# Moving a projection and early routing from the banks of the sum y to a transposing bank, in the first stage of an eight-layer kernel

## The reference, cut to what matters

```
xn = norm(norm(x)); u, z = split(xn @ W_in)
u2 = silu(conv(u)); dt, B, C = from(u2 @ W_xp)
for each of 16 states n and 256 channels e, along the 1024 tokens:
    h = exp(dt*A[e,n]) * h + (dt*u2)*B[n]        # a scan
    y += h * C[n]
y = (y + u2*D) * silu(z)
x = x + xn0 + res * (y @ W_out)                  # xn0: x normalised once
logits = norm(x) @ wg.T -> softmax, top groups, top 4 of 32 experts
```

## Time and profile before

| | us |
|---|---|
| three executions | 1595.17, 1598.65, 1599.42 |
| the profiled execution's own time | 1595.64 |
| its span (what the trace covers) | 1593.8 |
| the scan loop, first scan to the start of the last | 79.1 to 273.0 |
| VectorE busy in the span | 1022.7 |
| GpSimd busy in the span | 694.3 |
| TensorE busy in the span | 1259.4 |

### The profile page before, as it was taken

How to read it: one execution, slowest core, us unless ns; L and a number is a source line. 1 busy time by engine, 2 the same in 40 slices (tenths; PEclk the granted TensorE clock), 3 DMA queues, 4 the chain that set the end, 5 groups by cost and what they waited for, 6 DMA issues and landing times.

```text
span 1593.8 us, 27288 instructions
## 1 busy us (share of the span) xinstructions
PE 1259.4 (79%) x10086; PEld 895.2 (56%) x10086; DVE 1022.7 (64%) x1915; ACT 789.9 (50%) x1629; POOL 694.3 (44%) x688
## 2 busy tenths in 40 slices
PE   5888989322776568877868669998999999985996
PEld 2577768312554234444446534455776777874996
DVE  7798986760111888878743554547976885642775
ACT  3788685210433237767742235555665565321442
POOL 1099996474666340001014330024870881043453
PEclk9689999655888669999979889998999999997999
DMA  6388692112221431211001141112000003001113
GB/s 220 122 263 304 219 339 104 33 49 65 79 78 50 172 130 54 68 43 47 17 16 34 56 158 55 35 37 75 1 1 1 1 1 159 1 29 46 46 45 99
DMA packets 75492, 133.48 MB, mean 84 GB/s; under 512 B 12755, under 2 KB 39830, under 8 KB 74720
## 3 DMA queue, kind: packets, MB, share of 16 engines
q1 hardware_dynamic: 66432, 115.45, 22.1%
q0 software_dynamic: 8064, 13.87, 2.7%
q10 hardware_dynamic: 864, 2.43, 0.4%
HBM read 95.70 MB, written 38.38 MB: 84 GB/s over the span
## 4 chain that ended last, share of the span: by engine, by line
PE 47%; issue 18%; DVE 13%; ACT 7%; POOL 6%; DMA 4%; SPq 4%; another core or an unknown queue 1%; POOLq 0%; DVEq 0%; ACTq 0%
PE ps L1907 6%; PE ps L4138 3%; POOL sb_arena L1072 3%; PE ps L2274 2%; DVE sb_arena L1973 2%; ACT sb_arena L2221 2%; PE ps L2257 2%; PE ps L2516 1%; PE ps L3219 1%; PE ps L4105 1%; PE ps L4106 1%; PE ps L4107 1%; PE ps L3190 1%; SPq L68 1%
## 5 line engine op out<-in xcount | busy, mean ns | idle before, releaser
L1973 DVE TENSOR_REDUCE sb_arena<-ps 128x2 f32<-128x1024 f32 (+2 forms) x192 | 211.4, 1131 | 56.9 <-PE ps L2502 31.9
L2221 ACT ACTIVATE sb_arena<-ps 128x512 f32<-128x512 f32 (+1 forms) x320 | 160.3, 554 | 56.3 <-PE ps L2274 52.6
L889 DVE TENSOR_TENSOR_SCAN sb_arena<-ps,sb_arena 128x1024 f32<-128x1024 f32 x64 | 144.1, 2279 | 13.6 <-ACT ps L980 12.7
L2005 POOL CAST sb_arena<-sb_arena 128x8 bf16<-128x8 f32 (+2 forms) x32 | 6.5, 203 | 287.4 <-DVE sb_arena L1973 146.1
L1907 PE MATMUL ps<-sb_arena 128*32 128x256 f32 (+3 forms) x1856 | 115.1, 355 | 0.4 <-ACT sb_arena L2455 0.2
L1633 POOL DMA_INDIRECT y<-sb_arena x80 | 77.7, 972 | 55.7 <-ACT sb_arena L1582 32.9
L1173 POOL DMA_INDIRECT xe<-sb_arena x80 | 79.7, 996 | 49.9 <-issue 29.1
L1072 POOL TENSOR_TENSOR sb_arena<-sb_Wreg,sb_arena 128x1024 f32<-128x1024 f32 x32 | 74.8, 2365 | 59.9 <-DMA sb_arena<-bcrows 51.4
L705 PE MATMUL ps<-sb_const,sb_arena 128*128 128x128 f32 x768 | 92.3, 278 | 0.0
L705 PEld LDWEIGHTS ps<-sb_const,sb_arena 128*128 128x128 f32 x768 | 90.2, 195 | 2.0 <-issue 2.0
L2274 PE MATMUL ps<-sb_arena 51*128 51x256 bf16 (+2 forms) x768 | 60.7, 249 | 28.7 <-ACT sb_arena L2221 28.0
(11 more groups left out here) (526 smaller groups left out, 3491.0 us busy)
## 6 DMA issues: line engine op xcount, KB each, us to landing
sb_arena<-bcrows SPq DMA_DIRECT2D x80, 512.0 KB, 6.6
xe<-sb_one SPq DMA_DIRECT2D x31, 260.0 KB, 6.7
sb_Wreg<-e0w SPq DMA_DIRECT2D x24, 256.0 KB, 7.6
sb_arena<-xe SPq DMA_DIRECT2D x16, 325.0 KB
y<-sb_zero SPq DMA_DIRECT2D x20, 256.0 KB, 6.6
sb_arena<-y SPq DMA_DIRECT2D x4, 1024.0 KB, 8.9
sb_Wreg<-e1w SPq DMA_DIRECT2D x16, 256.0 KB, 2.8
sb_Wreg<-e3gu SPq DMA_DIRECT2D x1, 4096.0 KB, 14.2
```

What stands on the lines that cost most here:

```text
L889: e.tensor_tensor_scan(self.hh[i % 3], k.pair(2 * (i % 2)).rearrange("p c t -> p (c t)"), self.dB[i % 3], 0.0, MUL, ADD).then_inc(S.scan.s ...
L1973: e.tensor_reduce(dst, src, AX.X, MAX).then_inc(S.mxr.sem, 1)
L2221: e.activation(self.PT[s % 4][:, 2 * h:2 * h + 2, 0:n], bank[:, :, 0:n], ACT.Exp, scale=self.scale).then_inc(S.ex.sem, 1)
```

## The change

The projection of batch 0 is cut in two halves of four token tiles. Each half goes into bank 4, behind the first half of a transposed item: at i = 35 behind item 34 and at i = 39 behind item 38. VectorE takes each half out at i = 36 and i = 40. The next stage's turns (i = 47, 51) and logits (i = 55, 59) are cut in two in the same way and use bank 4. `turn_h` of items 36, 40, 48, 52, 56 and 60 waits until bank 4 has been read. `start_y` no longer waits for any of it. The signal `op` now counts three projections in place of two; the weights' wait in SyncE's queue goes from 1 to 2. The square root goes from i = 40 to 41, VectorE's part of the normalisation from 42 to 43, ScalarE's from 44 to 45.

```diff
@@ sp
                 w.wait_ge(S.gate, 2)
-                w.wait_ge(S.op, 1)
+                w.wait_ge(S.op, 2)
                 load_w_part(k, e, "e0", i - 38)
@@ turn_h
         before = i - 1 if i % 4 else i - 2
+        if i in (36, 40):
+            w.wait_ge(S.ox, (i - 32) // 4)
+        if i in (48, 52, 56, 60):
+            w.wait_ge(self.after.S.fxa, (i - 40) // 4)
         for c in range(2):
@@ start_y
         w.wait_ge(S.gate, g)
-        w.wait_ge(S.ox, b if eb == 0 else 0)
-        if g == 3:
-            w.wait_ge(self.after.S.fxa, 4)
@@ project_out becomes two functions
+    def project_first(self, e, w, c):
+        k, S = self.k, self.S
         w.wait_ge(S.g_wout, 16)
-        w.wait_ge(S.gate, 2 * b + 2)
+        w.wait_ge(S.gate, 2)
+        self.wait_half(w, 34 + 4 * c, 0)
+        for j in range(4 * c, 4 * c + 4):
+            for eb in range(2):
+                t = e.matmul(k.b(self.C)[:, (j % 4) * 128:(j % 4 + 1) * 128], self.sz[0][:, eb, j * 128:(j + 1) * 128], self.wout[:, eb, :],
+                             start=eb == 0, stop=eb == 1)
+        t.then_inc(S.op.sem, 1)
+    def project_last(self, e, w):    # as project_out(1) before, in banks 6 and 7
...
@@ pe, in the loop over i
             if n == 3 and i > 3:
-                w.wait_ge(S.gate, i // 16)
-                if i == 35:
-                    self.project_out(e, w, 0)
-                if i == 51:
-                    self.after.early_turns_pe(e, w)
-                    self.after.early_logits_pe(e, w)
                 self.start_y(e, w, i // 16)
+            if i in (35, 39):
+                self.project_first(e, w, (i - 35) // 4)
+            if i in (47, 51):
+                self.wait_half(w, i - 1, 0)
+                self.after.early_turns_pe(e, w, (i - 47) // 4)
+            if i in (55, 59):
+                self.wait_half(w, i - 1, 0)
+                self.after.early_logits_pe(e, w, (i - 55) // 4)
+            if n == 3 and i > 3:
                 self.add_y(e, w, i - 3)
             if i > 1 and (n != 2 or i == 2):
                 self.add_y(e, w, i - 2)
@@ out_dve becomes two functions
+    def out_first_dve(self, e, w, c):
+        k, S = self.k, self.S
+        xs = k.Xt[:, c * 512:(c + 1) * 512]
+        w.wait_ge(S.op, c + 1)
+        w.wait_ge(S.res, 16)
+        e.scalar_tensor_tensor(xs, k.b(self.C), k.s("res"), xs, MUL, ADD).then_inc(S.ox.sem, 1)
+        w.wait_ge(S.ox, c + 1)
+        tile_stats(k, e, w, range(4 * c, 4 * c + 4), S.stats if c else None)
...
@@ dve, in the loop over i
-            if i == 35:
-                self.out_dve(e, w, 0)
-            if i == 42:
+            if i in (36, 40):
+                self.out_first_dve(e, w, (i - 36) // 4)
+            if i == 43:
                 self.after.early_norm_dve(e, w)
@@ act, in the loop over i, behind decay(i + 2) and ahead of times_act(i)
-            if i == 40:
+            if i == 41:
                 self.after.deviations_act(e, w, 0)
-            if i == 44:
+            if i == 45:
                 self.after.early_norm_act(e, w)
-            if i == 51:
-                self.after.early_features_act(e, w)
-            if i == 52:
-                self.after.early_logits_act(e, w)
+            if i in (47, 51):
+                self.after.early_features_act(e, w, (i - 47) // 4)
+            if i in (55, 59):
+                self.after.early_logits_act(e, w, (i - 55) // 4)
...
```

More of the change, by code:

```diff
@@ L487, in __init__ @@
             B0=176, B1=176, B2=192, B3=192, B4=160, B5=160, C0=128, C1=128, hT=96, dA=64, dB=64, scan=64, hcv=16, hca=64, hcp=16, acc=64,
-            yd=4, gate=4, op=2, ox=2)
+            yd=4, gate=4, op=3, ox=3)
         k.g_x += [S.B2, S.B3]
@@ L491, in __init__ @@
         self.ready = (S.stats, 6)
-        self.ends = [(S.op, 2), (S.stats, 6), (S.res, 16), (S.dB, 64), (S.hcp, 16)]
+        self.ends = [(S.op, 3), (S.stats, 6), (S.res, 16), (S.dB, 64), (S.hcp, 16)]
     def two(self, v):
@@ L684, in start_y @@
         t.then_inc(S.yd.sem, 1)
-    def project_out(self, e, w, b):
+    def project_first(self, e, w, c):
         k, S = self.k, self.S
         w.wait_ge(S.g_wout, 16)
-        w.wait_ge(S.gate, 2 * b + 2)
+        w.wait_ge(S.gate, 2)
[7 more added lines that the diff above has]
+        k, S = self.k, self.S
+        w.wait_ge(S.gate, 4)
         for j in range(8):
             for eb in range(2):
-                t = e.matmul(k.b(self.Y + j // 4)[:, (j % 4) * 128:(j % 4 + 1) * 128], self.sz[b][:, eb, j * 128:(j + 1) * 128], self.wout[:, eb, :],
+                t = e.matmul(k.b(self.Y + j // 4)[:, (j % 4) * 128:(j % 4 + 1) * 128], self.sz[1][:, eb, j * 128:(j + 1) * 128], self.wout[:, eb, :],
                              start=eb == 0, stop=eb == 1)
@@ L764, in pe @@
         self.after.count_pe(e, w, 0)
-        self.project_out(e, w, 1)
+        self.project_last(e, w)
     def stats_dve(self, e, w, c):
@@ L843, in gate_dve, with out_last_dve @@
         e.tensor_tensor(self.two(zs), self.two(zs), k.pair(self.Y), MUL).then_inc(S.gate.sem, 1)
-    def out_dve(self, e, w, b):
+    def out_first_dve(self, e, w, c):
         k, S = self.k, self.S
-        xs = self.two(k.Xt[:, b * 1024:(b + 1) * 1024])
-        w.wait_ge(S.op, b + 1)
+        xs = k.Xt[:, c * 512:(c + 1) * 512]
+        w.wait_ge(S.op, c + 1)
         w.wait_ge(S.res, 16)
+        e.scalar_tensor_tensor(xs, k.b(self.C), k.s("res"), xs, MUL, ADD).then_inc(S.ox.sem, 1)
+        w.wait_ge(S.ox, c + 1)
+        tile_stats(k, e, w, range(4 * c, 4 * c + 4), S.stats if c else None)
+    def out_last_dve(self, e, w):
+        k, S = self.k, self.S
+        xs = self.two(k.Xt[:, 1024:2048])
+        w.wait_ge(S.op, 3)
         e.scalar_tensor_tensor(xs, k.pair(self.Y), k.s("res"), xs, MUL, ADD).then_inc(S.ox.sem, 1)
-        w.wait_ge(S.ox, b + 1)
-        tile_stats(k, e, w, range(8 * b, 8 * b + 8), S.stats)
+        w.wait_ge(S.ox, 3)
+        tile_stats(k, e, w, range(8, 16), S.stats)
     def dve(self, e, w):
@@ L900, in dve @@
         self.after.disp.dve(e, w, 0)
-        self.out_dve(e, w, 1)
+        self.out_last_dve(e, w)
         self.after.norm_dve(e, w)
@@ L1203, in __init__ @@
         self.S = S = k.signals(
-            g_w=16, stats=4, sd=2, rstd=3, xnv=8, tp=4, fxa=6, **dispatch_signals(4), lg=3, shift=4, probs=4,
+            g_w=16, stats=4, sd=2, rstd=3, xnv=8, tp=4, fxa=7, **dispatch_signals(4), lg=4, shift=4, probs=4,
             scat=1024, smg=4, smu=4, ssg=4, shs=4, sdn=4, sx=4,
@@ L1280, in features, with early_turns_pe, early_logits_pe @@
         return (self.early_xnT if c < 2 else self.xnT)[:, 512 * (c % 2):512 * (c % 2 + 1)]
-    def early_turns_pe(self, e, w):
-        k, S, Y = self.k, self.S, self.before.Y
+    def early_turns_pe(self, e, w, c):
+        k, S = self.k, self.S
         w.wait_ge(k.g_const, 16)
         w.wait_ge(S.fxa, 1)
[L1287 to L1292, removed]
+        for j in range(4):
+            t = e.transpose(k.b(self.before.C)[:, j * 128:(j + 1) * 128], self.early_xn[:, 4 * c + j, :], k.c("ident"))
+        t.then_inc(S.tp.sem, 1)
+    def early_logits_pe(self, e, w, c):
         k, S, E = self.k, self.S, self.E
-        w.wait_ge(S.fxa, 3)
-        for i in range(8):
-            t = e.matmul(k.b(self.before.Y)[:, i * E:(i + 1) * E], self.early_xnT[:, i * 128:(i + 1) * 128], k.s("wgT"), start=True, stop=True)
+        w.wait_ge(S.fxa, 2 + c)
+        for i in range(4 * c, 4 * c + 4):
+            t = e.matmul(k.b(self.before.C)[:, i % 4 * E:(i % 4 + 1) * E], self.early_xnT[:, i * 128:(i + 1) * 128], k.s("wgT"), start=True, stop=True)
         t.then_inc(S.lg.sem, 1)
@@ L1310, in logits_pe @@
         for c in (2, 3):
-            w.wait_ge(S.fxa, c + 3)
+            w.wait_ge(S.fxa, c + 4)
             for j in range(4):
@@ L1405, in route_dve @@
         if h < 2:
-            w.wait_ge(S.fxa, 4)
+            w.wait_ge(S.fxa, 5)
             w.all([(self.before.S.scan, 64), (self.before.S.hcv, 16), (self.before.S.hca, 64), (self.before.S.hcp, 16)])
         else:
-            w.wait_ge(S.lg, h)
+            w.wait_ge(S.lg, h + 1)
         w.mark(e.tensor_reduce(mx, l3, AX.X, MAX))
@@ L1534, in early_norm_act, with early_features_act, early_logits_act @@
         t.then_inc(S.fxa.sem, 1)
-    def early_features_act(self, e, w):
+    def early_features_act(self, e, w, c):
         S = self.S
[L1538 to L1542, removed]
+        w.wait_ge(S.tp, c + 1)
+        e.copy(self.features(c), self.k.b(self.before.C)).then_inc(S.fxa.sem, 1)
+    def early_logits_act(self, e, w, c):
         S = self.S
-        w.wait_ge(S.lg, 1)
-        e.copy(self.early_lg, self.k.b(self.before.Y)[:, 0:256]).then_inc(S.fxa.sem, 1)
+        w.wait_ge(S.lg, c + 1)
+        e.copy(self.early_lg[:, 128 * c:128 * c + 128], self.k.b(self.before.C)[:, 0:128]).then_inc(S.fxa.sem, 1)
     def features_act(self, e, w):
```

## The result

The change made the kernel slower: 1597.24 us, the median of 21 executions, against 1591.26 us for the kernel before (21 executions). The ratio is 1.0046, with a 95% interval of 1.0028 to 1.0063: 4.5 to 10.0 us, 7.3 in the middle; the two medians differ by 5.98. The forecast was +5.0 us, 1602.2 on the base that was then known; the base of these executions is lower, so the shift is what is compared. The profiled execution of the change took 1603.64 us (span 1601.8), that of before 1595.64 (span 1593.8).

A forecast was written before the change was run, and what follows sets the result against it. The prediction took GpSimd to pace the scan loop, so its idle times count. Terms -9.8 + 13.3 + 1.5 = +5.0 us, set on a mean of 1597.2, gave 1602.2 us, range 1594 to 1609.

The forecast's parts named there:

- The stall at 51: GpSimd's idle times from bank borrowing at item 51 go: 9.8 us gained, bounds 7 and 9.8.
- The release: SyncE's queue, held from load_b(39) on, is let go by the projection's second half at 197.2, 13.3 us later.
- What GpSimd pays: GpSimd waits for late B rows after dB(38), dB(42) at 213.7 not 200.33: 13.3 us lost, bounds 9 and 14.
- Crowding: Second-half statistics, square root, norm and ScalarE's tiles at items 40 to 45 delay scans 48, 49: 1.5 us lost, bounds 0 and 5.
- TensorE's clock: TensorE idles about 199 to 211 us and restarts slowly, up to 4 us, left within the bound of 5.
- The sum: Shift at the scan loop's end: -9.8 + 13.3 + 1.5 = +5.0 us, bounds -0.8 to +12.
- The rival that the release costs nothing: Op 2 comes before about 188 us and both stalls go: 12.7 us gained, 1584.5; chance 0.12 with partial forms.
- The wash: Same mechanism, loss at its lower bound through an earlier TensorE chain or quicker landing: 0 to +3 us, 1599; chance 0.30.
- The rival of crowding and slow restart: Slow-clock turns keep scans 41 to 50 behind, TensorE paces two or three periods: +8.5 us, 1605.7; chance 0.18.

The follow-up runs named there:

- routing_only: Kernel before with only the early routing (items 47 to 59) moved to bank 4, projection and normalisation left as they were; ratio 0.9942.
- projection_only: Kernel before with only the projection halves moved to bank 4, weights' wait at op 2, normalisation at 41, 43, 45; ratio 1.0103.
- change_late_norm44: change_late_weights with ScalarE's early normalisation at item 44 in place of 45; ratio to before 0.9925.
- change_late_weights: The whole change, with the weights' wait and 24 weight parts behind load_b(44) instead of load_b(38), some parts doubled; ratio to before 0.9934.
- routing_only_late_weights: routing_only with the weights' wait moved behind load_b(44) too; ratio to before 0.9930.
- change_wait_at_41: The change with the weights' wait behind load_b(41) in place of load_b(38), parts doubled at 41 to 43; ratio to before 0.9976.

## Why the prediction was right

**The stall at 51.** Forecast 9.8 us gained, 9.54 and 0.25. routing_only has 9.79 (9.81 from scan 35), but not by these two: the 9.54 us went, a gap of 0.24 stayed, and 0.84 stood in place of 1.08 and 2.47 ahead of the last product in place of 2.59.

**The release.** Forecast 13.3 us behind 183.93, out of TensorE's rows laid end to end: from the start of turn_h(34) to the release 18.2 us (178.98 to 197.2). Measured 177.99 to 196.5, 18.5 us, of which 0.44 was the wait for gate 2 that I had taken as 0. In projection_only, whose TensorE did not wait there, it was 178.88 to about 197.05, 18.2 us. The term is right to 0.3 us, and the 0.3 go with where VectorE stood.

**What GpSimd pays.** Forecast dB(38) to dB(42) 27.95 us; measured 27.03, against 14.58 before, a loss of 12.45 where 13.3 stood. The release came 12.1 us behind the start of dB(38), 0.6 more than forecast, so the term at fault is the landings: B(39) took 4.9 us in place of 5.3, and B(40) 6.6 in place of 8.0. I had carried over unchanged.

**Crowding.** Forecast 1.5 us; measured 0.65 + 1.76 = 2.4. The prediction had named four pieces, the half's statistics, the table loads, the norm and ScalarE's eight tiles, without a share for each. In change_late_norm44 the table loads carry 2.0 to 2.8 us and in change_late_weights the place of the eight tiles some more; how the 2.4 us of the change itself divide was not tried.

**TensorE's clock.** It stood still for 11.77 us and came back slow, 1.94 us for eight transposes that take 1.04, with a granted clock of 0.58 in this stretch:

```profile
200.00:210.00 10.00, 0.00 (x0) 0.00 (x0) 5.28 (x4) 1.81 (x2) 7.79 (x4) 0.57 1.01 359
210.00:216.00 6.00, 5.94 (x32) 5.97 (x33) 5.97 (x11) 2.95 (x4) 6.00 (x3) 0.58 1.03 413
216.00:230.00 14.00, 12.04 (x82) 9.32 (x80) 13.16 (x9) 12.65 (x30) 14.00 (x8) 1.00 0.99 382
```

GpSimd was busy 6.00 of the 6.00 us and 14.00 of the next 14.00. The gaps ahead of dB(53) and item 51's product stand also in change_late_weights (0.95 and 1.76), where TensorE stood still for 1.42 us at most between 182 and 240. So the slow restart was real, as the Trainium skill's "TensorE: Matmul & The Clock Gate", Part 1, has it, and cost nothing that reached the bound; I was right to leave it out of the sum.

**The sum.** -9.8 + 12.45 + 2.4 and 0.1 less ahead of the last product make +5.0, measured +5.01. That they agree to 0.01 is luck. Two terms were off by about 0.9 us each and cancelled, and up to 0.7 us of the measured 5.01 go with where VectorE stood in that one trace; without them it is +4.3. What the program as a whole lost, 4.5 to 10.0 us, takes in both. What was right is the mechanism: one stall gone, one made, and the second a little the larger. The rival that the release costs nothing was wrong at the point named for it: the release came at 196.5, 9.7 us behind the end of dB(38) at 186.8. The wash had a loss of 9 to 11 us, below what came. The rival of crowding and slow restart had 5 us for them, and 2.4 came.

## What to carry to other kernels

When a piece of work moves, follow the semaphore that it signals to every queue that waits for it, and ask what stands behind the wait there. Here the weights had time to spare and the B rows behind them had not: one wait placed six B rows later, with the weight parts doubled behind it, turns a loss of 5 us in the loop into a gain of 8.3 us. Before giving halves of a job to gaps, look at which half lets go of the queue.

The best kernels are change_late_norm44 (1584.35 us beside 1598.35, ratio 0.9925), routing_only_late_weights (0.9930) and change_late_weights (0.9934); their intervals overlap, also with routing_only's 0.9942. Counted from scan 35, routing_only has -9.81, routing_only_late_weights -9.76 and change_late_norm44 -9.67. As the square root now stands, the projection's move brings nothing on top of the routing's.

## What the runs showed of the hardware

- A VectorE instruction of 128 x 8 took from 0.14 to 5.00 us. Every one over 0.3 us that I followed ended within 0.07 us of the end of a GpSimd instruction, also 1.24 us in the kernel before and 1.77 in the changed one (at 219.03, to 220.80, where GpSimd's ended at 220.77). In two cases, 5.00 and 4.66 us, it waited through more than one. Not every small one does: the reciprocal at 205.33, with one input, took 0.18 us while GpSimd was busy until 205.91. The Trainium skill, "SBUF — State Buffer", section "Who interferes with whom", has the mechanism: VectorE and GpSimd share a pair of ports, held exclusively for a whole instruction, and a VectorE instruction with two inputs in SBUF needs it, as does a one-input `tensor_scalar` in some modes. The trace agrees for both forms, 2.28 and 4.66 us.
- The kernel before had medians of 1565.17, 1591.26 and 1598.35 us in the three sets. The first and the last set ran on the same chip by its number, so the chip is not shown to be the cause. The difference lies behind the loop: from the last product to the end of the span change_late_weights took 1281.9 us in the first set and change_wait_at_41 1329.2 in the last, while dB(1) to dB(38) took 106.56 and 106.54. What makes it stays open. Only ratios against executions beside it can be used.
- B rows behind one burst of loads took 4.9 and 6.6 us to land after 23 us of an empty queue, 5.3 and 8.0 after 10. Why they differ was not tried. Behind two doubled parts B(43) took 9.0 us.
